# Graph layer with gated attention and a mixture of experts: three small products in float32r with stacked high and low parts

## The chip, the cores and the metric

The kernel runs on one core of a Trainium2 chip. The metric is device time in microseconds; the time of the kernel before is 1862.65 us, the median of three runs (1862.06 to 1864.38).

## The reference, cut to what matters

6250 nodes of 256 features, 100,000 edges of 16 kinds, sorted by target; C = 256.

```
xn = layernorm(x)
gnn = segment_sum(einsum('ni,rio->rno', xn, weight)[rel_type, src] * norm, dst)
q, k, v = xn @ Wqkv ; k = softmax(k over nodes) ; context = k^T v per head (8 heads)
xm = layernorm(xn) * ln_g + ln_b
gate = sigmoid(gelu(xm @ Wg1 + bg1) @ Wg2 + bg2)      # Wg1 256x64, Wg2 64x256
x = x + gnn + (q @ context) * gate @ Wproj + bproj
tokens = layernorm(x)
probs = softmax(tokens @ router_w.T)                  # 8 experts
combine = top 2 of probs, divided by their sum
out = tokens
for e in range(8):
    out = out + combine[:, e] * (gelu(tokens @ w1[e] + b1[e]) @ w2[e] + b2[e])
x = x + out
```

## The kernel before

The nodes are cut into 49 tiles of 128. A large product is made in float32r from operands split into a high part (the value rounded to float32r) and a low part (the rest), as three passes high x high, low x high, high x low: the helper `three` (L1517 to L1526; its matmuls all bear L1524). Three small products are made in plain float32 instead, without a split, and a fourth uses `three`:

- GATES (L1661): the gate hidden `hgp` (64 rows) times `wg2`, two matmuls of 256 columns for a pair of tiles, each of which the trace records twice. It waits for `gap_dve` of the pair before, and ScalarE's GATE_ACT (L901) reads bank 5.
- COMBT and BIAS2 (L1692, L1700): the 8 combine weights of each node (`comb`) are transposed to 8 rows, copied to `ct` by ScalarE (L931), and multiplied with the expert biases `b2s`, one matmul of 256 columns for each tile of the pair, each recorded twice.
- LOGIT (L1685): the normalised tokens times the router, by `three`, six float32r matmuls of 8 columns for each tile. VectorE's TOP (L1403) copies the result out.

**First phase** (to about 900 us): a loop over the tiles. Per tile TensorE transposes the normalised tile, makes key and value (`kv_mm`), the gate's hidden product (64 columns, `hg_mm`), and eight blocks of relations (24 plus 24 matmuls of 512 columns, `gnn_mm`), which ScalarE and VectorE copy in turn to `stage` and SP writes to DRAM as `table`. VectorE scales the hidden product (L1201), ScalarE applies Gelu (L799), TensorE transposes the 64 columns (L1587), ScalarE copies them to `hgt` (L813), and SP stores `hgt` to `hg_d`, ahead of the store of the second half of the table. From tile 24 on, early rows of edges are gathered, split and summed beside it (L1564, L1565; VectorE L1169, L1175, L1190).

**Second phase** (the rest): 24 pairs of tiles and a last single one. All engines go through the same table of eight slots per pair, `SLOTS_OF_PAIR` (L1769): each entry names a step, and each engine carries out, in this order, the steps it has a function for. "+" belongs to the pair one behind, "-" to the pair two behind, "*" to the edges. In each slot TensorE does LAYER1 of one expert (twelve matmuls, `wreg` and `tt`), LAYER2 of another, two behind it (twelve, `ht` and `wreg`), and SUMS, six or four matmuls that sum edge messages (L1645 with the high, L1646 with the low parts). ScalarE makes the high parts of the messages (MSGS, L892), Gelu (L939) and the high part of LAYER1's result (L944). VectorE makes the selection (L1318), the low parts (L1332, L1437), and adds LAYER2's result to the accumulator (ADD, L1451). GATES stands at the end of slot 0, COMBT at the end of slot 2, BIAS2 at the end of slot 5, LOGIT in slot 6 ahead of SUMS. VectorE's COMB in slot 0 ends with L1425, which makes `comb`; in slot 4 MEAN and ScalarE's NORM (L913, L917) stand.

**Setup**: `b2s` and `wg2` are loaded as they are used; ScalarE splits other weights, then begins its first tile with the copies at L795.

## Time and profile before

| | |
|---|---|
| profiled execution | 1848.56 us |
| its span | 1847.0 us |
| TensorE busy | 1726.4 us, 93% |
| VectorE busy | 1352.7 us, 73% |
| ScalarE busy | 958.0 us, 52% |
| GpSimd busy | 1005.4 us, 54% |
| chain that ended last | TensorE 81% of the span, VectorE 5%, ScalarE 3%, issue 6% |

PE is TensorE's matmuls, DVE is VectorE, ACT ScalarE, POOL GpSimd, SP the engine that issues most transfers. Matmuls are pipelined: the duration of one is longer than the distance to the next, and the ends are modelled, so the pace of a block is read from the start of one block to the start of the next. Times in the rows are from the start of the span.

### The profile page before, as it was taken

What the parts mean: (1) busy time and instruction counts of PE and PEld (TensorE: products, weight loads), DVE (VectorE), ACT (ScalarE), POOL (GpSimd) and SP (SyncE); (2) the same over time, 40 slices, a digit from 0 to 9 for tenths busy, and PEclk for the clock granted to TensorE, in tenths of its full rate; (3) what the DMA queues carried; (4) which work ended last, traced back from release to release, by engine and by line L of the source; (5) the groups of instructions that cost most, each with busy time, mean ns of one, the idle gap of its engine ahead of it and who ended that gap; (6) DMA issues with size and microseconds to landing.
All of it is one profiled execution on the core that took longest, in us unless ns stands there. A gap on an engine that the chain in (4) does not pass through costs nothing.

```text
span 1847.0 us, 38898 instructions
## 1 busy us (share of the span) xinstructions
PE 1726.4 (93%) x10903; PEld 1526.2 (83%) x10903; DVE 1352.7 (73%) x3331; ACT 958.0 (52%) x2190; POOL 1005.4 (54%) x1132
## 2 busy tenths in 40 slices
PE   4999999989999999996679999999999999999998
PEld 3788888877778777775569999999999999999998
DVE  5767554466667666764678888888888888888885
ACT  3444222344444444443456666666666666666654
POOL 2233222577777777763366665656565656565630
PEclk9999999999999999997779999999999999999999
DMA  6565564566667666668633232333233333233320
GB/s 201 202 229 214 223 234 189 211 218 218 230 208 240 215 221 225 227 215 297 213 104 103 90 97 87 102 89 97 87 102 89 98 88 100 89 99 90 99 58 12
DMA packets 106583, 286.92 MB, mean 155 GB/s; under 512 B 19719, under 2 KB 41052, under 8 KB 93986
## 3 DMA queue, kind: packets, MB, share of 16 engines
q1 hardware_dynamic: 57762, 166.68, 24.3%
q0 software_dynamic: 40032, 110.39, 21.1%
q10 hardware_dynamic: 8736, 9.20, 1.6%
q8 instruction: 26, 0.43, 0.1%
q14 instruction: 27, 0.22, 0.0%
...
## 4 chain that ended last, share of the span: by engine, by line
PE 81%; issue 6%; DVE 5%; ACT 3%; ACTq 1%; another core or an unknown queue 1%; DMA 1%; DVEq 1%; POOL 0%; SPq 0%; POOLq 0%
PE bank L1524 65%; PE bank L1645 3%; PE bank L1646 2%; PE bank L1564 2%; PE bank L1565 2%; ACT mh L892 2%; PE bank L1706 1%; PE bank L1666 1%; DMA slot<-kv_d 1%; PE bank L1618 1%; ACTq L743 1%; DVE xtp L1372 1%; ACT raw L939 1%; PE bank L1681 1%
## 5 line engine op out<-in xcount | busy, mean ns | idle before, releaser
L709 POOL DMA_INDIRECT stg<-table,idxcur x495 | 507.6, 1025 | 375.6 <-PE bank L1646 189.8
L1524 PE MATMUL bank<-wreg,xt 128*128 128x512 f32 x2352 | 594.8, 404 | 13.6 <-issue 13.2
L1524 PEld LDWEIGHTS bank<-wreg,xt 128*128 128x128 f32 x2352 | 442.2, 193 | 114.0 <-issue 18.8
L609 POOL DMA_INDIRECT raw<-table,idxa x297 | 322.0, 1084 | 119.4 <-issue 72.4
L1524 PE MATMUL bank<-tt,wreg 128*128 128x256 f32 (+1 forms) x2400 | 320.6, 283 | 0.3 <-DVE tt L1398 0.3
L1524 PE MATMUL bank<-wreg,ht 128*128 128x256 f32 x2352 | 319.1, 284 | 0.0
L1524 PEld LDWEIGHTS bank<-tt,wreg 128*128 128x128 f32 x2400 | 298.3, 189 | 8.9 <-issue 6.8
L1524 PEld LDWEIGHTS bank<-wreg,ht 128*128 128x128 f32 x2352 | 294.7, 188 | 8.3 <-issue 8.3
L939 ACT ACTIVATE raw<-bank,cols 128x256 f32<-128x256 f32 (+1 forms) x400 | 163.8, 460 | 195.3 <-PE bank L1524 150.0
L1061 DVE COPY stg<-bank 128x512 f32<-128x512 f32 x196 | 133.9, 685 | 157.3 <-PE bank L1524 132.1
L1332 DVE SCALAR_TENSOR_TENSOR ml<-stg,nrm,mh 128x256 fp32r<-128x256 f32 x495 | 214.7, 480 | 36.7 <-ACT mh L892 33.3
L762 ACT COPY stg<-bank 128x512 f32<-128x512 f32 x196 | 113.1, 581 | 210.8 <-PE bank L1524 154.3
L892 ACT ACTIVATE mh<-stg,nrm 128x256 fp32r<-128x256 f32 x495 | 218.4, 498 | 4.7 <-DVE wreg L1022 1.1
L1451 DVE SCALAR_TENSOR_TENSOR xres<-bank,raw,xres 128x256 f32 (+1 forms) x392 | 170.2, 474 | 50.6 <-PE bank L1524 48.0
L1645 PE MATMUL bank<-mh,sel 128*128 128x256 f32 x495 | 158.3, 335 | 27.3 <-DVE ml L1332 25.3
L785 ACT ACTIVATE mh_a<-raw,nrm 128x256 fp32r<-128x256 f32 x297 | 129.2, 501 | 94.8 <-DMA raw<-table,idxa 71.5
L1437 DVE TENSOR_TENSOR ht<-raw,ht 128x512 fp32r<-128x512 f32 (+1 forms) x200 | 135.6, 678 | 27.2 <-ACT ht L944 27.2
L1175 DVE SCALAR_TENSOR_TENSOR ml_a<-raw,nrm,mh_a 128x256 fp32r<-128x256 f32 x297 | 129.1, 485 | 33.1 <-issue 21.3
L944 ACT CAST ht<-raw 128x512 fp32r<-128x512 f32 (+1 forms) x200 | 122.4, 612 | 38.5 <-PE bank L1524 30.0
L1646 PE MATMUL bank<-ml,sel 128*128 128x256 f32 x495 | 136.6, 287 | 0.0
L1645 PEld LDWEIGHTS bank<-mh,sel 128*128 128x128 f32 x495 | 95.6, 193 | 48.8 <-issue 17.7
L1524 PEld LDWEIGHTS bank<-wkvg,xt 128*128 128x128 f32 x588 | 97.2, 192 | 23.3 <-DVE xt L1065 5.1
...
## 6 DMA issues: line engine op xcount, KB each, us to landing
...
```

What stands on the lines that cost most here:

```text
L609: pool.indirect_dma_start(ring_a[:, r * EARLY + j, :], None, table[0:LIMIT, :], bass.IndirectOffsetOnAxis(ap=idxa[:, at:at + 1], axis=0)). ...
L709: pool.indirect_dma_start(stg[:, (s % 4) * SUP + j, :], None, table, bass.IndirectOffsetOnAxis(ap=idxcur[:, at:at + 1], axis=0)).then_inc( ...
L785: act.activation(mh_a[:, (r % 2) * EARLY + j, :], ring_a[:, r * EARLY + j, :], ACT.Copy, scale=nrm[:, bass.ds(EB * q + j, 1)]).then_inc(hi ...
L892: act.activation(mh[:, (s % 2) * CUT + j, :], stg[:, (s % 4) * SUP + j, :], ACT.Copy, scale=nrm[:, bass.ds(at + j, 1)]).then_inc(msg_hi, 1)
L939: act.activation(hf[e % 2][:, c * 256:c * 256 + nt * P], bank[2 + e % 2][:, c * 256:c * 256 + nt * P], ACT.Gelu, bias=b1c[:, 2 * e + c:2 * ...
L1061: dve.tensor_copy(stage[:, j // 4, (j % 4) * 512:(j % 4 + 1) * 512], bank[3 + j % 4][:]).then_inc(copied(k, j)[0], 1)
L1332: dve.scalar_tensor_tensor(out=ml[:, m, :], in0=stg[:, (s % 4) * SUP + j, :], scalar=nrm[:, bass.ds(at + j, 1)], in1=halves(mh[:, m, :]), ...
L1437: dve.tensor_tensor(ht[e % 2][:, LO, :, 0:n], cols2(hf[e % 2], n), halves(ht[e % 2][:, HI, :, 0:n]), ALU.subtract).then_inc(h_lo, 1)
L1451: dve.scalar_tensor_tensor(out=xk, in0=bank[6 + e % 2][:, a * C:(a + 1) * C], scalar=comb[:, a, e:e + 1], in1=xk, op0=ALU.mult, op1=ALU.ad ...
L1524: mm = pe.matmul(dst, stat(a, c), mov(b, c), start=(n == 0), stop=(n == 3 * chunks - 1))
L1645: pe.matmul(bank[u % 2][:, 0:C], sel[:, m, :], mh[:, m, :], start=(s % 2 == 0 and j == 0), stop=False)
L1646: mm = pe.matmul(bank[u % 2][:, 0:C], sel[:, m, :], ml[:, m, :], start=False, stop=(s % 2 == 1 and j == PART[1] - 1))
```

## The change

The three plain float32 products are made in float32r with split operands, and the router product with fewer matmuls.

- Gate: the hidden tile is doubled by Gelu into 128 columns (64 and the same 64 again), and transposed in one 128x128 transpose. ScalarE writes all 128 rows of `hgt` rounded; VectorE then overwrites rows 64 to 127 with value minus rounded value. `hg_d` and `hgp` have 128 rows. Wg2 is there as `wgh`, rounded, twice in rows, and `wgl`, its rest, 64 rows. GATES is `wgh` with all 128 rows (high and low of the hidden tile at once) and `wgl` with the high 64.
- Expert bias: `c3` holds high, low and high part of `comb` in columns 0, 32 and 64 of 96; COMBT transposes it to 96 rows; `b2h` holds the high part of the biases at rows 0 and 32 and the low part at row 64. BIAS2 is one float32r matmul of 96 rows per tile. New steps are COMB_HI (ScalarE, slot 0) and COMB_LOW (VectorE, the first of slot 1).
- Router: the high and low part of the router weights stand side by side, 16 columns; the high part of the tokens meets both in one matmul, the low part meets the high 8 columns. TOP sums the two halves while it reads them.

The core of the diff; declarations of tensors and semaphores and the renamed counts of waits are left out:

```diff
-            sp.dma_start(b2s[:], b2).then_inc(mixw_in, 16)
-            sp.dma_start(wg2[:], Wg2).then_inc(mixw_in, 16)
+            for n in range(3):
+                sp.dma_start(b2_raw[n * CW:n * CW + X, :], b2).then_inc(late_in, 16)
+            for n in range(2):
+                sp.dma_start(wg2_raw[n * G:n * G + G, :], Wg2).then_inc(late_in, 16)
...
-                act.activation(hgn[:, 1, :], hgn[:, 0, :], ACT.Gelu).then_inc(hg_act, 1)
+                act.activation(hgn[:, 1:3, :], hgn[:, 0:1, :].to_broadcast([P, 2, G]), ACT.Gelu).then_inc(hg_act, 1)
...
-                act.copy(hgt[b][:], bank[2][0:G, 0:P]).then_inc(hgt_cp, 1)
+                if not isinstance(i, int) or i > 0:
+                    act.wait_ge(hgt_cp, k - 1)
+                act.copy(hgt[b][:], bank[2][:, 0:P]).then_inc(hgt_hi, 1)
...
-            act.copy(rwh[:, HI], rwt[:]).then_inc(setup_act, 1)
-            act.wait_ge(mixw_in, 64)
+            act.copy(rwh[:, :, HI], rwt[:]).then_inc(setup_act, 1)
+            act.wait_ge(mixw_in, 32)
             act.copy(wproj[:, HI], wp_raw[:]).then_inc(setup_act, 1)
+            act.wait_ge(late_in, 5 * 16)
+            act.copy(wgh[:], wg2_raw).then_inc(setup_act, 1)
+            act.wait_ge(cleared, 4)
+            for n in range(2):
+                act.copy(b2h[n * CW:n * CW + X, :], b2_raw[n * CW:n * CW + X, :]).then_inc(setup_act, 1)
+            act.copy(b2h[2 * CW:2 * CW + X, :], b2_raw[2 * CW:2 * CW + X, :]).then_inc(setup_act, 1)
...
-                act.copy(ct[:, 0:nt * P], bank[5][0:X, 0:nt * P]).then_inc(ct_act, 1)
+                act.copy(ct[:, 0:nt * P], bank[5][0:3 * CW, 0:nt * P]).then_inc(ct_act, 1)
+
+            def COMB_HI(p, nt):
+                act.wait_ge(comb_dve, p + 1)
+                if not isinstance(p, int) or p > 0:
+                    act.wait_ge(ct_mm, p)
+                if isinstance(p, int) and p == 0:
+                    act.wait_ge(c3_clear, 1)
+                act.copy(c3[:, 0:nt, 0:3:2, 0:X],
+                         comb[:, 0:nt].unsqueeze(2).to_broadcast([P, nt, 2, X])).then_inc(c3_hi, 1)
...
+                dve.tensor_tensor(wgl[:], wg2_raw[0:G], halves(wgh[0:G]), ALU.subtract)
+                low = slice(2 * CW, 2 * CW + X)
+                dve.tensor_tensor(b2h[low, :], b2_raw[low, :], halves(b2h[low, :]), ALU.subtract)
...
+                dve.wait_ge(hgt_hi, k + 1)
+                dve.tensor_tensor(hgt[b][G:2 * G, :], bank[2][G:2 * G, 0:P], halves(hgt[b][G:2 * G, :]),
+                                  ALU.subtract).then_inc(hgt_cp, 1)
...
-                ch.link(dve, dve.tensor_copy(lg[:, 0:nt], bank[5][:, 0:nt * X].rearrange("p (a e) -> p a e", a=nt)))
+                got = bank[5][:, 0:nt * 2 * X].rearrange("p (a h e) -> p a e h", a=nt, h=2)
+                ch.link(dve, dve.tensor_reduce(lg[:, 0:nt], got, AX.X, ALU.add))
...
+            def COMB_LOW(p, nt):
+                dve.wait_ge(c3_hi, p + 1)
+                dve.tensor_tensor(c3[:, 0:nt, 1, 0:X], comb[:, 0:nt], halves(c3[:, 0:nt, 0, 0:X]),
+                                  ALU.subtract).then_inc(c3_lo, 1)
...
-                        pe.transpose(bank[2][0:G, 0:P], hgn[:, 1, :], ident[:]).then_inc(hgt_psum, 1)
+                        pe.transpose(bank[2][:, 0:P], hgn[:, 1:3, :].rearrange("p a g -> p (a g)"),
+                                     ident[:]).then_inc(hgt_psum, 1)
...
-                    mm = pe.matmul(bank[5][:, v * 256:v * 256 + n], wg2[:, v * P:(v + 1) * P],
-                                   hgp[:, 0:nt, :].rearrange("p a n -> p (a n)"), start=True, stop=True)
+                    pe.matmul(bank[5][:, v * 256:v * 256 + n], wgh[:, v * P:(v + 1) * P],
+                              hgp[:, 0:nt, :].rearrange("p a n -> p (a n)"), start=True, stop=False)
+                    mm = pe.matmul(bank[5][:, v * 256:v * 256 + n], wgl[:, v * P:(v + 1) * P],
+                                   hgp[0:G, 0:nt, :].rearrange("p a n -> p (a n)"), start=False, stop=True)
...
-                    mm = three(bank[5][:, a * X:(a + 1) * X], lambda h, c: tt[:, h, c, a * P:(a + 1) * P],
-                               lambda h, c: rwh[:, h, c, :])
+                    at = a * 2 * X
+                    for c in range(CC):
+                        pe.matmul(bank[5][:, at:at + 2 * X], tt[:, HI, c, a * P:(a + 1) * P],
+                                  rwh[:, c].rearrange("p h e -> p (h e)"), start=(c == 0), stop=False)
+                    for c in range(CC):
+                        mm = pe.matmul(bank[5][:, at:at + X], tt[:, LO, c, a * P:(a + 1) * P], rwh[:, c, HI, :],
+                                       start=False, stop=(c == CC - 1))
...
-                pe.wait_ge(comb_dve, p + 1)
+                pe.wait_ge(c3_lo, p + 1)
...
-                    mm = pe.transpose(bank[5][0:X, a * P:(a + 1) * P], comb[:, a, :], ident[:])
+                    mm = pe.transpose(bank[5][0:3 * CW, a * P:(a + 1) * P],
+                                      halves(c3[:, a].rearrange("p n e -> p (n e)")), ident[:])
...
-                    mm = pe.matmul(bank[4][:, a * C:(a + 1) * C], ct[:, a * P:(a + 1) * P], b2s[:],
+                    mm = pe.matmul(bank[4][:, a * C:(a + 1) * C], ct[:, a * P:(a + 1) * P], b2h[:],
                                    start=True, stop=True)
...
 SLOTS_OF_PAIR = (
-    ("-WEIGHT", "*SELECT", "-LOW 1", "*MSGS", "*WINDOW", "-COMB", "-LAYER1 2", "-LAYER2 0", "*SUMS", "+OUT",
+    ("-WEIGHT", "*SELECT", "-LOW 1", "*MSGS", "*WINDOW", "-COMB", "-COMB_HI", "-LAYER1 2", "-LAYER2 0", "*SUMS", "+OUT",
      "+GATES"),
-    ("*SELECT", "-ADD 0", "-LOW 2", "*MSGS", "+GATE_ACT", "+GATE", "-LAYER1 3", "-LAYER2 1", "+GATE_HI", "*SUMS"),
+    ("-COMB_LOW", "*SELECT", "-ADD 0", "-LOW 2", "*MSGS", "+GATE_ACT", "+GATE", "-LAYER1 3", "-LAYER2 1", "+GATE_HI", "*SUMS"),
```

Beside these, VectorE clears `b2h` in the setup (`cleared`) and `c3` once, and the spread of `kmax` (`kmb`) now lies in `dg`, which made it.

## Rows read from the trace of the kernel before

**Rows 1.** The page, part 1: busy us, share of the span, instructions of each engine.
```profile
PE 1726.4 (93%) x10903; PEld 1526.2 (83%) x10903; DVE 1352.7 (73%) x3331; ACT 958.0 (52%) x2190; POOL 1005.4 (54%) x1132
```

**Rows 2.** Stretches: us, PE, PEld, DVE, ACT, POOL busy (x), PEclk, DMA share, GB/s.
```profile
600.00:800.00 200.00, 186.12 (x915) 152.02 (x914) 137.04 (x313) 87.94 (x220) 150.22 (x147) 0.96 0.66 221
...
1300.00:1500.00 200.00, 198.42 (x1533) 186.95 (x1534) 173.12 (x461) 130.21 (x300) 122.31 (x133) 1.00 0.32 95
```

**Rows 3.** Order of time, TensorE, one pair: start, us, line, operation, [idle before].
```profile
1275.96 1.13 PE L1706 MATMUL bank<-b2s,raw 8*128 8x256 f32 x4
1277.02 1.70 PE L1524 MATMUL bank<-wreg,ht 128*128 128x256 f32 x12
1278.55 1.58 PE L1524 MATMUL bank<-tt,wreg 128*128 128x256 f32 x12
1279.97 1.40 PE L1524 MATMUL bank<-rwh,tt 128*128 128x8 f32 x12
1281.23 0.36 PE L1645 MATMUL bank<-mh,sel 128*128 128x256 f32 x1
...
1290.69 1.13 PE L1666 MATMUL bank<-hgp,wg 64*128 64x256 f32 x4
1291.75 1.70 PE L1524 MATMUL bank<-tt,wreg 128*128 128x256 f32 x12
1293.28 1.60 PE L1524 MATMUL bank<-wreg,ht 128*128 128x256 f32 x12
...
1298.46 0.38 PE L1645 MATMUL bank<-mh,sel 128*128 128x256 f32 x1 [0.25 <-DVE ml L1332]
...
1299.88 1.68 PE L1524 MATMUL bank<-wproj,xtp 128*128 128x256 f32 x12
1301.40 0.38 PE L1697 MATMUL bank<-ident,raw 128*8 128x128 f32 x2
1301.54 1.68 PE L1524 MATMUL bank<-tt,wreg 128*128 128x256 f32 x12
...
1312.87 1.13 PE L1706 MATMUL bank<-b2s,raw 8*128 8x256 f32 x4
```

**Rows 4.** The same pair on VectorE.
```profile
1282.39 0.69 DVE L1437 TENSOR_TENSOR ht<-raw,ht 128x512 fp32r<-128x512 f32 x1 [0.35 <-ACT ht L944]
...
1286.60 0.69 DVE L1437 TENSOR_TENSOR ht<-raw,ht 128x512 fp32r<-128x512 f32 x1 [0.43 <-ACT ht L944]
...
1290.39 0.18 DVE L1425 TENSOR_TENSOR raw<-raw 128x16 f32<-128x16 f32 x1
...
1291.67 0.68 DVE L1437 TENSOR_TENSOR ht<-raw,ht 128x512 fp32r<-128x512 f32 x1
...
1293.30 0.69 DVE L1367 SCALAR_TENSOR_TENSOR scr<-gate,bank 128x512 f32<-128x512 f32 x1 [0.16 <-ACT gate L901]
1295.59 0.88 DVE L1451 SCALAR_TENSOR_TENSOR xres<-bank,raw,xres 128x256 f32 x2 [1.61 <-PE bank L1524]
...
1311.48 0.91 DVE L1332 SCALAR_TENSOR_TENSOR ml<-stg,nrm,mh 128x256 fp32r<-128x256 f32 x2 [0.70 <-ACT mh L892]
```

**Rows 5.** The same pair on ScalarE.
```profile
1288.06 0.81 ACT L939 ACTIVATE raw<-bank,cols 128x256 f32<-128x256 f32 x2
...
1292.43 0.84 ACT L901 ACTIVATE gate<-bank,small 128x256 f32<-128x256 f32 x2 [2.09 <-PE bank L1666]
```

**Rows 6.** Order of time, TensorE, in a tile of the first phase.
```profile
252.05 0.38 PE L1533 MATMUL bank<-ident,xn 128*128 128x128 f32 x2
252.27 0.27 PE L1587 MATMUL bank<-ident,hgn 128*64 128x128 f32 x1
252.30 5.85 PE L1524 MATMUL bank<-wreg,xt 128*128 128x512 f32 x24
```

**Rows 7.** Order of time in the setup, ScalarE.
```profile
37.87 1.05 ACT L762 COPY stg<-bank 128x512 f32<-128x512 f32 x2
```

**Rows 8.** The same, TensorE.
```profile
40.22 7.39 PE L1524 MATMUL bank<-wreg,xt 128*128 128x512 f32 x24
```

More of the change, by code:

```diff
@@ L115, in gps_layer @@
         kmax = sb("kmax", [P, C], F32)
-        kmb = sb("kmb", [P, C], F32)
-        wg2 = sb("wg2", [G, C], F32)
+        wgh = sb("wgh", [2 * G, C], F32R)
+        wgl = sb("wgl", [G, C], F32R)
         cols = sb("cols", [P, 32], F32)
         rwt = sb("rwt", [P, CC, X], F32)
-        rwh = sb("rwh", [P, 2, CC, X], F32R)
-        b2s = sb("b2s", [X, C], F32)
+        rwh = sb("rwh", [P, CC, 2, X], F32R)
+        b2h = sb("b2h", [3 * CW, C], F32R)
         iota8 = sb("iota8", [P, X], F32)
@@ L138, in gps_layer @@
             kvs = [sb(f"kvs{b}", [P, KVW], F32, one) for b in range(2)]
-            hgn = sb("hgn", [P, 2, G], F32, one)
-            hgt = [sb(f"hgt{b}", [G, P], F32, one) for b in range(2)]
+            hgn = sb("hgn", [P, 3, G], F32, one)
+            hgt = [sb(f"hgt{b}", [2 * G, P], F32R, one) for b in range(2)]
             bpb = sb("bpb", [P, C], F32, one)
@@ L288, in gps_layer @@
         hgt_psum = sem("hgt_psum")
+        hgt_hi = sem("hgt_hi")
         hgt_cp = sem("hgt_cp")
@@ L1248, in _ @@
             dve.memset(xres[96:P, NT - 1, :], 0.0).then_inc(cleared, 1)
+            dve.memset(halves(b2h[:]), 0.0).then_inc(cleared, 1)
             for k in range(K2):
@@ L1271, in shifts @@
                     dve.wait_ge(kv_in[s], 16 * i + 16)
-                    dve.tensor_tensor(slot[:, s, 0:C], slot[:, s, 0:C], kmb[:], ALU.subtract).then_inc(k_shift, 1)
+                    dve.tensor_tensor(slot[:, s, 0:C], slot[:, s, 0:C], dg[:], ALU.subtract).then_inc(k_shift, 1)
             dve.wait_ge(flag_ready, 1)
@@ L1480, in slot_of @@
                 in_slot(i, s, groups, p1, n1, p2, n2, SELECT=SELECT, MSGS=MSGS, WINDOW=WINDOW, LAST_WINDOW=LAST_WINDOW, GATE=GATE,
-                        GATE_LOW=GATE_LOW, STATS=STATS, MEAN=MEAN, TURN_LOW=TURN_LOW, TOP=TOP, COMB=COMB,
+                        GATE_LOW=GATE_LOW, STATS=STATS, MEAN=MEAN, TURN_LOW=TURN_LOW, TOP=TOP, COMB=COMB, COMB_LOW=COMB_LOW,
                         BIAS2_ADD=BIAS2_ADD, LOW=LOW, ADD=ADD)
```

37 lines of the change are left out of this document (22 added, 15 removed).

## The prediction

> **What bounds the kernel now.** I read the page first, then the table of stretches, then the order of time on TensorE, VectorE and ScalarE inside one pair of the second phase. The reader is to see that TensorE is busy 93% of the span [rows 1], that in a stretch of the second phase it is at 198.4 of 200 us while VectorE is at 173.1 and ScalarE at 130.2, and that in a stretch of the first phase with early sums it is at 186.1 with VectorE at 137.0 [rows 2]. The clock column is 1.00 in the second phase, so its 2.4 GHz level holds and I look for no clock effect there. So the second phase is TensorE's. It takes 36.91 us for a pair of tiles (BIAS2 starts at 1275.96 and next at 1312.87 [rows 3]), and there are 24.5 pairs. But TensorE is not alone at the limit: six SUMS matmuls that start at 1298.46 take until 1299.88, 1.42 us, after an idle 0.25 us, because VectorE's low parts come late [rows 3]. VectorE in its turn idles where TensorE or ScalarE is late: 0.35, 0.43 and 1.61 us [rows 4]. A saving on TensorE counts only if these hand-overs move with it, so both are worked out.
>
> **The change part by part, second phase.** The yardstick is the float32r matmul of 256 columns: twelve from 1278.55 to 1279.97, 0.118 us each [rows 3].
> BIAS2: two plain float32 matmuls (four records) from 1275.96 to 1277.02, 1.06 us; the twelve behind them take 1.53 where 1.42 is usual, 0.11 more, so 1.17 [rows 3]. After: two float32r matmuls of the same 256 columns with 96 rows instead of 8, 0.24. The trace has none of 96 rows; its bounds are 0.24 (as fast as any of 128 rows) and 1.06 (nothing won), and I take the first, to which every float32r row is nearest. Saved 0.93.
> GATES: 1290.69 to 1291.75, 1.06, and 1.53 for the twelve behind, 1.17 in all [rows 3]. After: four float32r matmuls, 0.47. Saved 0.70, bounds 0 and 0.70.
> LOGIT: twelve of 8 columns take 1.26 us, 0.105 each [rows 3], nearly what 256 columns cost, so the load of 128x128 weights sets the pace and not the columns. After: eight with the same loads, 16 columns in four of them. Saved 4 x 0.105 = 0.42; bounds 0 (if 16 columns cost twice 8) and 0.42.
> COMBT: two transposes in 0.14 [rows 3] with 8 weight columns. After: 96 weight columns; two transposes with 128 weight columns take 0.22 [rows 6]. Cost 0 to 0.1, taken at 0.05.
> The sum on TensorE is 0.93 + 0.70 + 0.42 - 0.05 = 2.0 us per pair.
> A rule bears on the first two terms. The trace gives 0.53 us for one float32 matmul of 256 columns. The Trainium skill, "FP8 and Floating Point Precision", TensorE Precision Notes, has true float32 as four passes, and "TensorE: Matmul & The Clock Gate", Architectural detail and Back-to-back issue gap, has a pass at 256/2.4 + 2.5 ns; an estimate from these is 0.44 us, by which BIAS2 would save 0.64 and GATES 0.41, and the sum 1.4 instead of 2.0. The rows decide for 2.0.
>
> **Does it pass the other engines?** I walk one pair with VectorE.
> Up to SELECT of slot 7 nothing on VectorE moves. It then waits 0.35 at L1437 (1282.39) and 0.43 (1286.60) for ScalarE's high parts of experts 0 and 1 [rows 4]; those follow LAYER1 0 and 1, which start 0.93 and 1.35 us earlier, so both waits go, and VectorE reaches COMB 0.8 us earlier.
> There the change adds a chain. COMB's last instruction starts at 1290.39 and takes 0.18 [rows 4]; new are COMB_HI on ScalarE and COMB_LOW, which is VectorE's first instruction of slot 1. VectorE stands idle through ScalarE's copy and two hand-overs. Bounds are 0.2 (that op alone, like the 0.18) and 0.7 (the longest wait for ScalarE in these rows, 1311.48); I take 0.3 of idleness and 0.17 for the subtraction, 0.45 in all. Queued behind the waiting VectorE are SELECT, ADD 0, LOW 2 and the messages of slot 1, and SUMS waits for them. Queued behind ScalarE's COMB_HI are LAYER1 2, the messages of slot 1 and the gate. LAYER1 2 ran at 1288.06, 2.3 us before COMB's last op [rows 4, 5]. COMB now ends at 1290.57 - 0.8 = 1289.8, so LAYER1 2 starts near 1290.0; its Gelus take 0.81 [rows 5] and the high part some 0.6, so that is there near 1291.4. VectorE's LOW 2 started at 1291.67 [rows 4] and comes at 1291.67 - 0.8 + 0.45 = 1291.3, so it waits about 0.1. The gate ran at 1292.43 after a wait [rows 5]; GATES now ends about 2 us earlier, and the gate follows ScalarE's messages, near 1292.3. So this chain costs VectorE 0.45 to 0.65 and takes nothing from TensorE in slots 0 and 1, which needs expert 2's parts only in slot 2.
> Then ADD 1: VectorE is free at 1293.98 (0.69 after 1293.30), and waits 1.61 for LAYER2 1 to 1295.59 [rows 4]. TensorE is 2.0 us earlier there, so ADD 1 starts at 1293.6 if TensorE decides, and at 1293.98 - 0.8 + 0.45 + 0.1 = 1293.7 if VectorE does: both arrive together, 1.9 to 2.0 earlier. From there to the end of slot 5 VectorE had nearly no wait for TensorE, only 0.70 for ScalarE's messages behind NORM (1311.48 [rows 4]), so the rest of the pair moves as a block. The replacement of TOP's copy by a sum over two halves adds 16 elements to a small op, under 0.05. The memory of c3 and the use of dg for kmb are once per run.
> So what TensorE saves passes, with no reserve: 2.0 us per pair. Late next are the SUMS of slot 2 and PROJ, which wait for VectorE as they do now. Over 24.5 pairs this is 49 us.
>
> **First phase.** The gate hidden transpose has 128 weight columns instead of 64. Now it starts 0.22 after the pair ahead of it and the next block starts 0.03 behind it [rows 6], so its weight load hides; I take 0, bounds 0 and 0.08 per tile. ScalarE's Gelu doubles from 64 to 128 columns: hidden, ScalarE is at 88 of 200 [rows 2]. VectorE gets one subtraction of 64x128 from PSUM behind kmax, between the 0.18 of 16 columns (1290.39) and the 0.69 of 512 (1293.30) [rows 4], about 0.3; behind it on VectorE are the early rows and two evacuations, for which TensorE waits. In the first 24 tiles TensorE is saturated and VectorE idle enough. In the 25 tiles with early sums TensorE already loses 7% [rows 2]; bounds are 0 and 0.3 for each, and I take 0.13: 3 us. SP's stores come in the same number; the one of hg_d is twice as wide and waits for VectorE, ahead of the second table store, which is not due until later in the tile.
> Setup: ScalarE gets wgh and three copies for b2h, behind a wait for VectorE's last memsets of the setup; so its table copies of 37.87 come near 41 [rows 7]. TensorE's block at 40.22 needs them, but has 7.39 us for 24 matmuls [rows 8] that take 5.85 elsewhere [rows 6], since VectorE holds it up; so 1.5 of some 3 us are covered, the bounds are 0 and 3, and I take 1. SP issues five small transfers for two ahead of the edge lists, with no one late behind them.
> First phase: +4 us, bounds 0 and 14 (0.08 x 49 + 0.3 x 25 + 3).
>
> **The sum.** The profiled execution took 1848.56 us (span 1847.0). 1848.56 - 49 + 4 = 1803.6. The median of the runs shown is 1862.65, 0.76% above it; in that proportion the forecast is **1817 us**.
>
> **Rivals.**
> A: the hand-over of the combine weights costs more. For it: VectorE arrives at ADD 1 with no reserve, so each further 0.1 us in COMB_HI, LOW 2 or the gate counts in full. Against it: the ops are small. With 1 us lost per pair (the upper bound of the idleness, 0.4 above what I take, and the same again at LOW 2 and the gate), the gain is 24.5 x 1.0 - 4 = 20 us, near 1842.
> B: more than the direct sum comes back. ScalarE waits 2.09 us for the gate and VectorE 1.61 us at ADD 1 just behind the float32 GATES [rows 4, 5], though TensorE's record of LAYER2 1 ends at 1293.28 + 1.60 = 1294.9 [rows 3]; if such late hand-overs hang on the float32 work, SUMS of slot 2 with its 0.7 us too many and 0.25 idle shortens as well. 3.0 us per pair gives 1848.56 - 73 + 4 = 1779.6, near 1793.
> C, the other side: ScalarE's queue. COMB_HI holds LAYER1 2, the messages and the gate for the 2.3 us between 1288.06 and COMB's end. If ScalarE cannot make it up and arrives that much later with the gate, ADD 1 and all behind it, the full 2.3 us fall on the pair against 2.0 saved: +0.3 x 24.5 + 4 = +11, near 1874. It decides once more than about 2 us of the hold reach ADD 1. Against it: ScalarE idled 2.09 us ahead of the gate [rows 5], which takes the hold up.
> D: float32 matmuls cost only the four passes (the 1.4 us per pair above): 1848.56 - 34 + 4, near 1832. Here the mechanism would be that the rest of the 0.53 us is a cost of switching kinds that stays with the remaining float32 transposes; the 0.11 us behind BIAS2 speaks for a switching cost, but of that size only.
>
> **How the numbers follow.** Forecast 0.62, A 0.17, B 0.12, D 0.05, C 0.04. The range reaches from B to just beyond A, 1793 to 1845; what is left out are C and gains above 3 us per pair. Faster by over 0.2% (3.7 us, about what a measurement of this kernel can tell from no change) holds in all but C and a sliver of A: 0.94; same 0.02, slower 0.04.
>
> **What would show it.** BIAS2 start to BIAS2 start at 34.9 us; two BIAS2 records about 0.24 us long together, four GATES in 0.47, eight LOGIT in 0.84, and 1.42 for the block behind each; an idle 0.3 us on VectorE ahead of c3's subtraction; the waits at 1282.39, 1286.60 and 1295.59 gone or under 0.3; ScalarE's L939 of expert 2 behind COMB_HI; VectorE busy over 90% of a second phase stretch. A pair of 36 us, or a VectorE wait of a microsecond in slot 1, would make the prediction wrong on A's side; a first phase that ends 10 us later would break the term of 4 us.

## The result, and the profile after

On the chip of the first measurement the changed kernel took 1852.64 us (median of 4, 1851.96 to 1855.34) beside 1863.52 for the kernel before (median of 4, 1862.06 to 1866.85): 0.9942 of it, 95% interval 0.9925 to 0.9959. That is 0.6% faster, 11 us, where 2.4% or 46 us was predicted; the time lies 8 us above the range. On three further chips the same kernel took 0.985, 0.9851 and 0.9838 of before. So there are two gaps to explain: from 2.4% to 1.5%, which all chips share, and from 1.5% to 0.6%, which only the first chip shows.

The profiled execution took 1855.34 us (span 1853.6). The page's part 1, which answers [rows 1]:
```profile
PE 1706.4 (92%) x10756; PEld 1512.4 (82%) x10756; DVE 1368.3 (74%) x3409; ACT 963.8 (52%) x2219; POOL 1032.9 (56%) x1132
```
TensorE has 20 us less to do, yet in a stretch of the second phase it is now idle for 6 of 200 us, where before it was idle for 1.6 [rows 2]; VectorE's share has not risen. The stretch (columns as in [rows 2]):
```profile
1300.00:1500.00 200.00, 193.85 (x1508) 183.54 (x1508) 172.95 (x469) 129.80 (x305) 127.43 (x131) 1.00 0.33 98
```
One pair on TensorE, in order of time, the blocks that answer [rows 3] (the blocks on line 1564 stand for line 1524 of before):
```profile
1288.95 0.41 PE L1755 MATMUL bank<-b2h,ct 96*128 96x256 f32 x2
1289.19 1.59 PE L1564 MATMUL bank<-wreg,ht 128*128 128x256 f32 x12
1291.60 1.67 PE L1564 MATMUL bank<-tt,wreg 128*128 128x256 f32 x12 [0.81 <-DVE tt L1431]
1293.11 0.28 PE L1733 MATMUL bank<-rwh,tt 128*128 128x16 f32 x2
...
1293.91 0.36 PE L1686 MATMUL bank<-mh,sel 128*128 128x256 f32 x1
...
1303.39 0.28 PE L1707 MATMUL bank<-hgp,wgh 128*128 128x256 f32 x1
1303.60 0.38 PE L1709 MATMUL bank<-hgp,wgl 64*128 64x256 f32 x1
1303.91 0.38 PE L1707 MATMUL bank<-hgp,wgh 128*128 128x256 f32 x1
1304.23 0.38 PE L1709 MATMUL bank<-hgp,wgl 64*128 64x256 f32 x1
1304.54 1.68 PE L1564 MATMUL bank<-tt,wreg 128*128 128x256 f32 x12
1306.05 1.61 PE L1564 MATMUL bank<-wreg,ht 128*128 128x256 f32 x12
...
1325.59 0.41 PE L1755 MATMUL bank<-b2h,ct 96*128 96x256 f32 x2
```
BIAS2 takes 0.24 us (1288.95 to 1289.19) and LOGIT 0.80 (1293.11 to 1293.91), as predicted. (COMBT, the transpose of `c3`, is still plain float32: the change turns two of the plain products into float32r, GATES and BIAS2, and reorders the router's.) GATES takes 1.15 (1303.39 to 1304.54) where 0.47 was predicted and 1.06 stood before. LAYER1 0 waits 0.81 us for TURN_LOW, a wait that did not exist. VectorE in the same pair, with two new waits (1289.52 is ADD 5, 1308.92 is ADD 1):
```profile
1289.52 0.88 DVE L1490 SCALAR_TENSOR_TENSOR xres<-bank,raw,xres 128x256 f32 x2 [0.97 <-PE bank L1564]
1290.32 0.55 DVE L1351 TENSOR_TENSOR sel<-dbl,dpr 128x384 fp32r<-128x384 f32 x1
1290.78 0.68 DVE L1431 TENSOR_TENSOR tt<-bank,tt 128x512 fp32r<-128x512 f32 x1
...
1303.58 0.17 DVE L1463 TENSOR_TENSOR c<-raw,c 128x16 fp32r<-128x16 f32 x1 [0.36 <-ACT c L956]
...
1308.92 0.88 DVE L1490 SCALAR_TENSOR_TENSOR xres<-bank,raw,xres 128x256 f32 x2 [1.67 <-PE bank L1564]
```
The hand-over of the combine weights costs 0.36 + 0.17 us, near the 0.45 predicted. ADD 1's wait, 1.61 before [rows 4], is still there with 1.67, and ADD 5, ahead of TURN_LOW in VectorE's order, has a new one of 0.97. Both follow a TensorE block that had been over for long by its record: LAYER2 5 ran from 1286.91 for 1.68 us, to 1288.59, and ADD 5 starts 0.93 us after that; LAYER2 1 ends at 1306.05 + 1.61 = 1307.66, and ADD 1 starts 1.26 us after that. ScalarE, in the same pair:
```profile
1303.33 0.22 ACT L956 CAST c<-raw 128x32 fp32r<-128x32 f32 x1 [2.52 <-issue]
1303.51 0.84 ACT L965 ACTIVATE raw<-bank,cols 128x256 f32<-128x256 f32 x2
```

### The profile page after: what moved, and what is told of

It reads as the page before. It is cut to its first block, busy times and chain, and to the rows that moved or that the text cites. A ratio compares the mean times of both kernels' runs of the same rounds, so it can differ in the third digit from the quotient of the medians.

```text
span 1853.6 us, 38739 instructions
## 1 busy us (share of the span) xinstructions
PE 1706.4 (92%) x10756; PEld 1512.4 (82%) x10756; DVE 1368.3 (74%) x3409; ACT 963.8 (52%) x2219; POOL 1032.9 (56%) x1132
## 4 chain that ended last, share of the span: by engine, by line
PE 74%; DVE 8%; issue 8%; ACT 3%; DMA 2%; POOL 2%; another core or an unknown queue 1%; ACTq 1%; DVEq 1%; SPq 0%; POOLq 0%
PE bank L1564 60%; PE bank L1686 3%; PE bank L1604 2%; PE bank L1687 2%; PE bank L1605 2%; DMA slot<-kv_d 1%; DVE ml L1365 1%; ACT mh L909 1%; POOL raw L618 1%; ACTq L752 1%; DVE sel L1351 1%; PE bank L1659 1%; DVE xres L1490 1%; DVE xtp L1405 1%
## 5 line engine op out<-in xcount | busy, mean ns | idle before, releaser
L718 POOL DMA_INDIRECT stg<-table,idxcur x495 | 531.5, 1074 | 347.3 <-PE bank L1687 123.4
```

The lines of the kernel that those rows point to most:

```text
L718: pool.indirect_dma_start(stg[:, (s % 4) * SUP + j, :], None, table, bass.IndirectOffsetOnAxis(ap=idxcur[:, at:at + 1], axis=0)).then_inc( ...
```

## The experiments

Sixteen runs were made in four groups, each group on a chip of its own with the kernel before beside it. The kernel before took 1863.5 us on the first chip, 1851.1, 1773.6, 1775.2 and 1850.4 on the second to the fifth, so only ratios are compared across chips. The pair is the distance of two BIAS2 blocks, over 21 pairs of the profile (of the kernel before, 36.87 on the first chip). One execution of each run was profiled.

| kernel | chip | median us | of before [95%] | pair us |
|---|---|---|---|---|
| the changed kernel | 1 | 1852.64 | 0.9942 [0.9925, 0.9959] | 36.59 |
| turn_low_first | 2 | 1826.11 | 0.9873 [0.9846, 0.9900] | 35.79 |
| bias_float32 | 2 | 1825.98 | 0.9862 [0.9836, 0.9889] | 35.95 |
| gate_rows_128 | 2 | 1817.17 | 0.9817 [0.9791, 0.9843] | 35.55 |
| router_alone | 2 | 1836.05 | 0.9911 [0.9882, 0.9940] | 36.13 |
| changed_again | 3 | 1746.91 | 0.9850 [0.9828, 0.9872] | 34.60 |
| first_phase_only | 3 | 1779.41 | 1.0035 [1.0020, 1.0050] | 35.90 |
| gate_float32 | 3 | 1740.88 | 0.9818 [0.9795, 0.9841] | 34.26 |
| select_first_padded | 3 | 1746.34 | 0.9845 [0.9822, 0.9867] | 34.65 |
| changed_third | 4 | 1747.81 | 0.9851 [0.9829, 0.9873] | 34.61 |
| gate_undone | 4 | 1746.77 | 0.9841 [0.9827, 0.9854] | 34.60 |
| gate_rows_again | 4 | 1738.99 | 0.9789 [0.9776, 0.9802] | 34.18 |
| turn_low_again | 4 | 1757.10 | 0.9892 [0.9877, 0.9908] | 35.15 |
| gate_padded | 5 | 1830.34 | 0.9889 [0.9867, 0.9911] | 35.84 |
| small_padded | 5 | 1824.71 | 0.9856 [0.9832, 0.9880] | 35.66 |
| changed_fourth | 5 | 1820.95 | 0.9838 [0.9815, 0.9860] | 35.62 |
| turn_low_third | 5 | 1824.40 | 0.9841 [0.9815, 0.9867] | 35.73 |

**Is it the order ADD 5, SELECT, TURN_LOW?** turn_low_first, turn_low_again and turn_low_third are one kernel:
```
-    ("-ADD 5", "*SELECT", "+TURN_LOW", "-LOW 7", "*MSGS", ...
+    ("*SELECT", "+TURN_LOW", "-ADD 5", "-LOW 7", "*MSGS", ...
```


> The changed kernel with one line of the slot table changed: in slot 6 VectorE does SELECT and TURN_LOW ahead of ADD 5 instead of ADD 5 ahead of both. Theory H (a hand-over took the place of the float32 time): LAYER1 0 waits for TURN_LOW, which stands on VectorE behind ADD 5, and ADD 5 waits for the signal of LAYER2 5; without that the block of LAYER2 6 shrinks from 2.21 us (mean of 20 pairs) to 1.45, a pair goes from 36.6 to 35.8-36.1 us, and the time from 1852.6 to 1834-1842. Rival C (VectorE and ScalarE are simply full, the order does not matter): the pair stays within 0.1 of 36.6 and the time within 3 us of 1852.6.

> The changed kernel with SELECT and TURN_LOW ahead of ADD 5, again, beside the changed kernel itself on one chip. Theory H: it is faster than the changed kernel, by 0.5 to 0.9 us a pair where LAYER1 0 waited (late signals), by nothing elsewhere. Theory L: on a chip with prompt signals it is the same within 0.1% or slower by up to 0.3 us a pair, since MSGS of slots 6 and 0 come later behind TURN_LOW's own wait of 0.8 us.

> The changed kernel with SELECT and TURN_LOW ahead of ADD 5. Where signals are prompt it is slower than the changed kernel by 0.5 us a pair (35.15 against 34.60, 0.9892 of before). On a chip where before takes 1850 or more: Theory H says 0.5 to 0.9 us a pair faster than the changed kernel beside it, since LAYER1 0's wait goes; Theory L says the same loss as elsewhere, and the gap between its 0.9873 and the changed kernel's 0.9942 was the chips'.

The first run looked like a success beside the first chip's 0.9942. Beside the changed kernel on one chip it is none: 0.9892 against 0.9851 on the fourth, 0.9841 against 0.9838 on the fifth, where its pair is 0.11 us longer and Theory L had expected the fourth chip's 0.5. VectorE stands idle at TURN_LOW where it would have done ADD 5; fourth chip, VectorE:
```profile
1074.05 0.55 DVE L1351 TENSOR_TENSOR sel<-dbl,dpr 128x384 fp32r<-128x384 f32 x1
1075.40 0.69 DVE L1431 TENSOR_TENSOR tt<-bank,tt 128x512 fp32r<-128x512 f32 x1 [0.80 <-ACT tt L940]
```
The delay is then in slot 7, where SUMS takes 0.89 us instead of 0.47 (mean of 19 pairs, to the next block's start). So Theory H's cure fails. Its wait is real on every chip, though: the changed kernel on the fourth chip, TURN_LOW on VectorE, then LAYER1 0 on TensorE:
```profile
1209.60 0.68 DVE L1431 TENSOR_TENSOR tt<-bank,tt 128x512 fp32r<-128x512 f32 x1
```
```profile
1210.41 1.69 PE L1564 MATMUL bank<-tt,wreg 128*128 128x256 f32 x12
```
LAYER1 0 starts 0.13 us after TURN_LOW ends. LAYER2 6 ahead of it takes 1.62 instead of the usual 1.42 to 1.44, and LAYER1 0 itself 1.52 instead of 1.41: 0.3 us a pair. With the first chip's late LAYER2 5 this grows to the 0.81 of the pair above.

**The gate product.** gate_rows_128 and gate_rows_again are one kernel, which gives Wg2's low part 128 rows too:
```
-        wgl = sb("wgl", [G, C], F32R)
+        wgl = sb("wgl", [2 * G, C], F32R)
...
-                dve.tensor_tensor(wgl[:], wg2_raw[0:G], halves(wgh[0:G]), ALU.subtract)
+                dve.tensor_tensor(wgl[:], wg2_raw, halves(wgh[:]), ALU.subtract)
...
-                                   hgp[0:G, 0:nt, :].rearrange("p a n -> p (a n)"), start=False, stop=True)
+                                   hgp[:, 0:nt, :].rearrange("p a n -> p (a n)"), start=False, stop=True)
```


> The changed kernel with the low part of Wg2 on all 128 rows, so that all four matmuls of GATES have 128 rows (the added product is low x low, negligible). Theory G: the 0.31 us each of the four comes from the alternation of 128 and 64 rows; now they take 0.12 each, GATES 0.47 instead of 1.15. If TensorE's time in slot 0 passes, the pair falls by 0.68 and the time by 17 to 1836; under H most of it is lost again to the hand-overs in slots 2 and 6, the pair falls by 0-0.3 and the time by 0-8. Rival: the 0.31 us is the price of this product whatever its rows, GATES stays at 1.15 and nothing moves.

> The changed kernel with Wg2's low part on 128 rows times the full stacked hidden layer, again, beside the changed kernel itself on one chip. It took 0.9817 of before on the second chip, with GATES at 0.47 us. Theory S: GATES 1.15 to 0.47, the next block 0.1 less, pair 0.7 to 0.8 shorter than the changed kernel's, so 17 to 19 us: ratio to before 0.975, my predicted 0.9755, where signals are prompt. Rival C (VectorE sets the pair once TensorE has this little): pair at most 0.35 shorter, as in float32 with 128 rows, ratio 0.981, with TensorE waiting for VectorE somewhere.

The added product, low times low, changes no time but its own. The weight loads (PEld) of GATES in changed_third:
```profile
1221.97 0.19 PEld L1707 LDWEIGHTS bank<-hgp,wgh 128*128 128x128 f32 x1
1222.30 0.18 PEld L1709 LDWEIGHTS bank<-hgp,wgl 64*128 64x128 f32 x1
1222.61 0.19 PEld L1707 LDWEIGHTS bank<-hgp,wgh 128*128 128x128 f32 x1
```
The matmuls of the same GATES:
```profile
1222.09 0.28 PE L1707 MATMUL bank<-hgp,wgh 128*128 128x256 f32 x1
1222.30 0.38 PE L1709 MATMUL bank<-hgp,wgl 64*128 64x256 f32 x1
1222.61 0.38 PE L1707 MATMUL bank<-hgp,wgh 128*128 128x256 f32 x1
```
In gate_rows_again, the weight loads:
```profile
1049.56 0.19 PEld L1709 LDWEIGHTS bank<-hgp,wgl 128*128 128x128 f32 x1
1049.68 0.19 PEld L1707 LDWEIGHTS bank<-hgp,wgh 128*128 128x128 f32 x1
```
and the matmuls:
```profile
1049.56 0.28 PE L1707 MATMUL bank<-hgp,wgh 128*128 128x256 f32 x1
1049.68 0.28 PE L1709 MATMUL bank<-hgp,wgl 128*128 128x256 f32 x1
1049.79 0.28 PE L1707 MATMUL bank<-hgp,wgh 128*128 128x256 f32 x1
```
With one row count a load starts a matmul ahead of its own (1049.56 for the matmul of 1049.68) and matmuls follow at 0.12 us. Where the row count changes, load and matmul start together (both 1222.30, both 1222.61) and matmuls follow at 0.31. GATES is then 0.46 us long (1049.56 to 1050.02), just the term of the sum. It is the change of the row count that costs, and not the 64 rows: in the kernel before, the four records of GATES start 0.32, 0.22 and 0.22 us apart, and in gate_float32 below, on 128 rows, 0.22, 0.22 and 0.22. Once the first is through, 64 rows follow each other as fast as 128.

With the 0.1 us that the block behind gets shorter, 0.78 us are saved on TensorE; 0.43 reach the pair (34.61 to 34.18) and 9 us the time. This is rival C of that expectation in part: SUMS of slot 2 takes 1.07 us instead of 0.75 (mean of 19 pairs), since it now waits for VectorE, which has no wait of its own from 1052.92 on. TensorE's SUMS and PROJ in gate_rows_again:
```profile
1056.57 0.28 PE L1687 MATMUL bank<-ml,sel 128*128 128x256 f32 x1
1056.74 0.38 PE L1686 MATMUL bank<-mh,sel 128*128 128x256 f32 x1
1056.97 0.28 PE L1687 MATMUL bank<-ml,sel 128*128 128x256 f32 x1
1057.35 1.68 PE L1564 MATMUL bank<-wproj,xtp 128*128 128x256 f32 x12
```
and VectorE's messages there:
```profile
1055.43 1.26 DVE L1365 SCALAR_TENSOR_TENSOR ml<-stg,nrm,mh 128x256 fp32r<-128x256 f32 x3
1056.62 0.68 DVE L1405 TENSOR_TENSOR xtp<-scr,xtp 128x512 fp32r<-128x512 f32 x1
```
This kernel is the fastest of its group on both chips: 0.9789 of before on the fourth (the changed kernel 0.9851) and 0.9817 on the second.

gate_float32 has the same 128 stacked rows in plain float32, and leaves Wg2's low part out of the product:
```
-                    pe.matmul(bank[5][...], wgh[...], hgp[:, 0:nt, :]..., start=True, stop=False)
-                    mm = pe.matmul(bank[5][...], wgl[...], hgp[0:G, 0:nt, :]..., start=False, stop=True)
+                    mm = pe.matmul(bank[5][...], halves(wgh[...]), halves(hgp[:, 0:nt, :]...), start=True, stop=True)
```


> The changed kernel with GATES as two plain float32 matmuls of 128 rows (stacked Wg2 high against stacked high and low parts of the hidden layer); Wg2's low part is left out of the product. The bias product in float32 on 96 rows took 0.68 us for two (0.34 each), where the kernel before paid 1.06 for two of 8 rows and 1.06 for two of 64 rows (0.53 each). Theory R (a float32 matmul of 256 columns costs 0.53 us on 64 rows or fewer and 0.34 on more): GATES takes 0.68 to 0.75 us instead of 1.15, the pair falls by 0.4 to 36.2 us, time 0.98 to 0.99 of before. Rival Q (float32 costs four passes whatever the rows, 0.42 to 0.53 us each, and the 0.34 came from the next block's start): GATES takes 0.9 to 1.06 us and the time is that of the changed kernel.

TensorE, its GATES and the matmul behind:
```profile
1015.04 1.02 PE L1707 MATMUL bank<-hgp,wgh 128*128 128x256 f32 x4
1015.72 0.47 PE L1564 MATMUL bank<-tt,wreg 128*128 128x256 f32 x1
```
From the start of GATES to the end of the matmul behind it are 1.15 us here, 1.45 in the kernel before on 64 rows (1290.69, and 1291.75 + 0.39), 1.52 in changed_third (1222.09, and 1223.23 + 0.38). So plain float32 on full rows beats the changed form, and the pair shows it (34.26 against 34.60). The next start at 0.68 flatters it, as rival Q has it: four records span 1.02 with the last at 0.38, so they follow at 0.215 us, 0.43 for one float32 matmul. The Trainium skill, "FP8 and Floating Point Precision", TensorE Precision Notes, has true float32 as four passes, from which the prediction estimated 0.44; by that rule, the trace agrees. What the 0.53 of before had on top was the switch of the row count, 128 to 64 or 8 and back.

bias_float32 and select_first_padded (the padded gate weights, the reordering above, and this second one):
```
-                    mm = pe.matmul(bank[4][...], ct[:, a * P:(a + 1) * P], b2h[:], ...
+                    mm = pe.matmul(bank[4][...], halves(ct[:, a * P:(a + 1) * P]), halves(b2h[:]), ...
```
```
-    ("-ADD 1", "*SELECT", "-LOW 3", ...
+    ("*SELECT", "-ADD 1", "-LOW 3", ...
```


> The changed kernel with BIAS2's two matmuls in plain float32 again on the same 96 rows (everything else of the change kept). BIAS2 grows from 0.24 to 1.06 us and the block behind it by 0.1. Theory H: this only fills the time in which LAYER1 0 waits for TURN_LOW, so the pair stays at 36.5-36.9 and the time within 6 us of 1852.6, and LAYER2 5's signal reaches VectorE early again. Rival D (the saving of BIAS2 had passed in full and something else grew): the pair grows by 0.9 us and the time by 22 to 1875.

> The changed kernel with three edits: Wg2's low part on 128 rows with the full stacked hidden layer, SELECT and TURN_LOW ahead of ADD 5 in slot 6, SELECT ahead of ADD 1 in slot 2. Theory H+G (the two losses are separate and add): GATES 0.47 us, LAYER2 6 1.46 us, LAYER2 2 under 1.7 us, so 35.54 (gate weights on 128 rows) less 0.15 and less 0.3 to 0.5: a pair of 35.0 us, time 0.976 of before. Rival C (VectorE, busy 31 of 35.5 us with its own small gaps, sets the pair): 35.5 us and 0.982, as with the gate weights alone; VectorE's wait ahead of ADD 1 or TURN_LOW only moves.

bias_float32 has no changed kernel beside it, so neither of its rivals can be judged by the time; its pair is 0.4 longer than gate_rows_128's. Its BIAS2 starts 0.68 us before the next block, where 1.06 was expected on 96 rows: this miss led to gate_float32. select_first_padded comes out at the changed kernel's time (0.9845 and 0.9850): the two reorderings together lose what the gate weights win. Which of the two loses is not shown there; turn_low_again alone loses 0.54 a pair.

**The parts.** router_alone is the kernel before with the LOGIT and TOP edits. first_phase_only is the kernel before with the first phase's share of the gate edit; its GATES leaves out the low part of the hidden layer. gate_undone takes the whole gate edit back; the core of its diff:
```
-        hgt = [sb(f"hgt{b}", [2 * G, P], F32R, one) for b in range(2)]
+        hgt = [sb(f"hgt{b}", [G, P], F32, one) for b in range(2)]
...
-                act.activation(hgn[:, 1:3, :], hgn[:, 0:1, :].to_broadcast([P, 2, G]), ACT.Gelu).then_inc(hg_act, 1)
+                act.activation(hgn[:, 1, :], hgn[:, 0, :], ACT.Gelu).then_inc(hg_act, 1)
```


> The kernel before with the router part of the change alone (eight matmuls instead of twelve, VectorE sums two halves). LOGIT 1.26 -> 0.81 us. Theory H: nothing in slots 6, 7 and 0 waits for late parts any sooner than before, LAYER1 0 does not start earlier, so the saving passes: pair 36.9 -> 36.5, time 5 to 11 us below the kernel before. Rival C (the other engines are full): pair unchanged, time within 3 us of before.

> The kernel before with only the first-phase part of the gate edit: Gelu written twice, a transpose of 128 columns, the stacked copy to hgt, VectorE's subtraction of rows 64 to 127 and its wait for ScalarE's copy, and stores and loads of 128 rows of hgt. GATES still multiplies rows 0 to 63 in float32, now the rounded high part, so the low part of the hidden gate layer is left out of the output. My prediction put this part at +4 us (bounds 0 and +14). If it holds: ratio 1.002 with tile 12 about 2 us and the last tile about 4 us later than before, the second phase unchanged at 36.85 us a pair. Rival F (the wait for ScalarE's copy and 128-row stores cost more, and are what the changed kernel loses): +10 us or more, ratio 1.005 or more. Rival Z: nothing, 1.000 +- 0.002.

> The changed kernel with the whole gate edit undone: Wg2 and the hidden layer in float32 on 64 rows again, no doubled Gelu, no stacked copy, no subtraction in the first phase, 64-row stores and loads; bias product and router stay changed. Theory S (terms add, TensorE sets the pair): GATES 1.15 to 1.06 us, pair 0.1 us shorter than the changed kernel's, first phase 4 to 6 us shorter: 6 to 9 us below the changed kernel, ratio to before 0.980 to 0.982 on a chip with prompt signals. Then the gate edit as written is a loss. Rival T (the first phase's cost is hidden, GATES no dearer than before where the data comes from): within 2 us of the changed kernel.

The router edit alone gives 0.9% [0.6, 1.2] on the second chip, more than its 0.42 us a pair (10 us, 0.55%): the pair is 0.7 shorter than before's on the first chip, but no pair of before was profiled on the second. The first phase's share costs 0.35%, 6.2 us, with an interval of 3.5 to 8.9.

Undoing the whole gate edit leaves the pair as it is (34.60 and 34.61). The reason stands on TensorE, in OUT (`xtp` and `wqc`), the block just ahead of GATES; gate_undone, then changed_third, whose GATES starts at 1222.09 as shown above:
```profile
1215.21 1.57 PE L1554 MATMUL bank<-xtp,wqc 128*128 128x256 f32 x12
1216.72 1.13 PE L1697 MATMUL bank<-hgp,wg 64*128 64x256 f32 x4
```
```profile
1220.68 1.57 PE L1564 MATMUL bank<-xtp,wqc 128*128 128x256 f32 x12
```
Ahead of a GATES that begins with 64 rows OUT takes 1.51 us, ahead of one that begins with 128 it takes 1.41. That gives back the 0.09 by which GATES itself is longer (1.15 against 1.06). So the gate edit gains nothing on TensorE. Whether the first phase's cost then remains, the medians do not tell: they are 1.0 us apart (0.9841 and 0.9851), with intervals of 2.4 and 3.9 us to either side, too wide to tell rival T's 2 us from Theory S's 6. The profiled executions are 5.9 us apart, 5.5 of them before the first BIAS2 (926.2 against 931.7).

**Prompt and late hand-overs.** changed_again, changed_third and changed_fourth are the changed kernel unedited.

> The changed kernel itself, unedited, on the chip of the runs beside it. On its first chip it took 0.9942 of the kernel before. Three of its edited copies took 0.9873 (TURN_LOW ahead of ADD 5), 0.9862 (bias product in float32) and 0.9817 (gate weights on 128 rows) on a second chip. Theory H (it loses time in its own order of waits, at LAYER1 0 behind TURN_LOW): the same kernel shows the same here, 0.994 +- 0.003, pairs of 36.6 us that swing by 1.5 us, LAYER1 0's wait ahead of it, and so a time clearly above those copies. Rival N (what set it apart was the chip or the one profiled execution): a ratio of 0.987 or less, steady pairs near 35.9 us and no wait ahead of LAYER1 0.

> The changed kernel unedited, beside the three below. So far: 0.9942 of before on a first chip (pairs of 36.6 us against 36.87), 0.985 on a third chip, where both kernels ran 5% faster (pairs of 34.60 against 35.89). In the third chip's traces every semaphore signal of TensorE came about 0.3 us behind its block; in those of the first, behind a third of the blocks, it came 0.6 to 4 us behind. Theory L (late signals of TensorE, and nothing in the kernel's order, take the rest of the gain): if the time of before is near 1773 us here, signals are prompt and the ratio is 0.985 with steady pairs; if it is near 1850 to 1863, signals are late and the ratio is 0.988 to 0.994. Theory H (the order ADD 5, SELECT, TURN_LOW): LAYER1 0 waits for TURN_LOW on any chip.

> The changed kernel unedited, as baseline of this chip. If before takes about 1773 us: 0.985, pairs of 34.60 us. If before takes 1850 or more: signals of TensorE up to 4 us late, pairs of 36 to 36.6 us, ratio 0.988 to 0.994.

On the fourth chip, ADD 1 and ADD 5 on VectorE (LAYER2 1 and 5 on TensorE start at 1224.74 and 1241.23 there and take 1.61 and 1.69), and the stretch:
```profile
1226.50 0.88 DVE L1490 SCALAR_TENSOR_TENSOR xres<-bank,raw,xres 128x256 f32 x2 [0.40 <-PE bank L1564]
```
```profile
1243.05 0.88 DVE L1490 SCALAR_TENSOR_TENSOR xres<-bank,raw,xres 128x256 f32 x2 [0.17 <-PE bank L1564]
```
```profile
1300.00:1500.00 200.00, 199.88 (x1597) 193.02 (x1595) 183.13 (x502) 137.69 (x321) 135.66 (x141) 1.00 0.35 104
```
ADD 1 and ADD 5 start 0.15 and 0.13 us after the blocks' recorded ends, where on the first chip it was 1.26 and 0.93. What VectorE waited for TensorE ahead of all ADDs (us, times), over 22 pairs: the kernel before and the changed kernel on the first chip, then the changed kernel on the fifth and on the fourth:
```profile
  PE bank L1524: 30.8, 39
```
```profile
  PE bank L1564: 33.2, 33
  remote: 11.2, 6
```
```profile
  PE bank L1564: 13.9, 36
```
```profile
  PE bank L1564: 9.4, 35
```
So with prompt hand-overs TensorE is full (199.9 of 200 us) and VectorE at 91.6%. The semaphores' events in the traces show the same: over 21 pairs, of those that could be matched, 28% of TensorE's signals in the kernel before and 33% in the changed one came more than 0.5 us after the recorded end of the matmul that gives them, and 31% in changed_fourth; on the third and fourth chip none did.

The mean of 19 pairs, us from a block's start to the next block's, shows where the pair gets longer (the number behind a name is the chip):

| | before, 1 | changed, 1 | first_phase_only, 3 | changed_again, 3 | changed_fourth, 5 | gate_padded, 5 |
|---|---|---|---|---|---|---|
| LAYER2 6, up to LAYER1 0 | 1.54 | 2.20 | 1.54 | 1.61 | 1.61 | 1.56 |
| OUT | 1.50 | 1.56 | 1.50 | 1.41 | 1.43 | 1.41 |
| GATES | 1.06 | 1.16 | 1.06 | 1.15 | 1.15 | 0.67 |
| LAYER2 2 and SUMS, slot 2 | 3.21 | 3.25 | 2.19 | 2.19 | 2.85 | 3.36 |

Slot 2 loses 1.0 us on the first chip, before the change as much as after it, and nothing on the third. Of what only the changed kernel loses on the first chip, the largest part is 0.6 us ahead of LAYER1 0. There ADD 5 starts 0.77 us after LAYER2 5's recorded end in the mean; in the kernel before, and in changed_fourth, it is 0.14.

The fifth chip is as slow as the first for the kernel before within 0.7%, and still the changed kernel gets 0.9838 there. Rival N of that expectation holds: the 0.9942 was met on one chip of four, and is not the kernel's order alone. Of Theory L the prompt side holds; its late side (0.988 to 0.994) fails on the fifth chip, where signals are late and the ratio is 0.9838.

**Padding alone.** gate_padded is gate_undone with rows of zeros from 64 to 128 in Wg2 and in the hidden layer's buffer; small_padded is router_alone with the same and with the bias product's operands padded from 8 to 96 rows, nothing stacked:
```
-        wg2 = sb("wg2", [G, C], F32)
+        wg2 = sb("wg2", [2 * G, C], F32)
...
-        b2s = sb("b2s", [X, C], F32)
+        b2s = sb("b2s", [3 * CW, C], F32)
```


> The changed kernel with the gate edit undone, and Wg2 and the hidden layer's buffer of the second phase padded with rows of zeros from 64 to 128, cleared once: the product is the float32 one of the kernel before, on 128 rows. Theory R (a float32 matmul of 256 columns takes 0.53 us on 64 rows and 0.34 on 128): GATES 0.67 where the 64-row form takes 1.06, pair 34.2 to 34.3, without the first phase's doubled work: where signals are prompt 8 us below the changed kernel, ratio to before 0.979 to 0.981. Rival Q (the 0.34 came from the data, zeros and the like, or VectorE sets the pair below 34.6): GATES 1.06, or GATES 0.67 and a pair still of 34.6, and a time within 2 us of the changed kernel.

> The kernel before with the router edit, and with its two small float32 products merely padded with zero rows (gate product to 128 rows, bias product from 8 to 96): nothing is split into high and low parts, no hand-over of the combine weights, no work added to the first phase. Theory R: BIAS2 0.68 instead of 1.06 and 0.24 in the changed kernel, GATES 0.67, LOGIT 0.81; TensorE's sum is before's less 0.38, 0.39 and 0.44 = 1.2 us a pair, 34.7 us, and VectorE and ScalarE have 0.45 and 0.22 us less to do than in the changed kernel: ratio to before 0.983 to 0.985, as much as the changed kernel got. Rival C (VectorE's work sets the pair): below 34.5 us and faster than the changed kernel.

BIAS2 of small_padded and the matmul behind it, on TensorE:
```profile
1016.68 1.03 PE L1722 MATMUL bank<-b2s,ct 96*128 96x256 f32 x4
1017.36 0.47 PE L1533 MATMUL bank<-wreg,ht 128*128 128x256 f32 x1
```
From BIAS2's start to the end of the next matmul are 1.15 us, as in gate_float32, where the 8-row form of before takes more: its next matmul only starts after 1.06 [rows 3]. So the direction of Theory R holds for 8 rows too; its price of 0.34 does not, since the block behind two such matmuls gets 0.19 us longer (its second matmul starts 0.30 after its first instead of 0.12).
The times do not settle more: small_padded, with no splitting, no hand-over and no first phase work, is within the interval of the changed kernel (0.9856 and 0.9838), and gate_padded is slower (0.9889) though it does less: its GATES has 0.67, and slot 2 takes 3.36 us where changed_fourth has 2.85 (table above). Neither Theory R's 0.979 to 0.981 nor rival Q's equal time came. Both ran only on the fifth chip, where a good part of the hand-overs is late; what padding is worth where they are prompt is not shown.

## Why the prediction was wrong

- **BIAS2 and LOGIT**: right. 0.24 and 0.80 us where 0.24 and 0.84 were predicted, and 96 rows count as 128 do. What the walk missed is that the 0.93 saved brings TensorE to LAYER1 0 before TURN_LOW is done, even on the chips with prompt hand-overs: 0.3 us a pair.
- **GATES**: the step that failed everywhere. The term "after: four float32r matmuls, 0.47, saved 0.70" was mis-sized: it measured 1.15, because two of the four have 64 rows between neighbours of 128, and with the 0.09 that OUT gets shorter it saves nothing. gate_rows_again has the 0.46. With 128 rows throughout the time falls by 9 us, half of the 17 that lie between 2.4% and 1.5%; the other half does not pass VectorE (next point).
- **"What TensorE saves passes, with no reserve"**: right where hand-overs are prompt. The sum with GATES corrected is 2.0 - 0.7 = 1.3 us a pair; measured between the third chip's first_phase_only, whose second phase is the kernel before's in time, and changed_again: 35.90 - 34.60 = 1.30. That they agree to the hundredth is luck: the 0.3 at LAYER1 0 is made up by several savings under 0.1 us each that the sum did not have, as in the block ahead of BIAS2 (0.61 and 0.53). It ends soon after: with 0.78 less on TensorE, 0.43 arrive, and VectorE's slot 2 decides.
- **ADD 1's wait "goes"**: nearly right where hand-overs are prompt: in the mean of 19 pairs it falls from 1.27 us (first_phase_only) to 0.34 (changed_again), the rest being what GATES failed to save. It failed on the first chip (1.37 and 1.42). The walk moved ADD 1's start by what TensorE saves ahead of it, and so took the time between TensorE's recorded end and VectorE's start for constant. It was 0.7 us before (1295.59 against 1294.9, [rows 4] and [rows 3]) and is 1.26 after, in the mean 0.79 and 1.20. With the order ADD 5, SELECT, TURN_LOW a late LAYER2 5 reaches LAYER1 0 (0.81 us). The pair fell by 0.28 instead of 1.3. The first chip's share of the miss is thus located, but its cause is not shown.
- **Hand-over of the combine weights**: 0.36 of idleness for 0.3, 0.17 as taken. The two waits at L1437 are gone. Rivals A and C fell; ScalarE still idles 2.52 ahead of COMB_HI.
- **Rival B**: the excess of SUMS in slot 2 does not hang on the float32 work. first_phase_only has the float32 GATES and BIAS2 and no excess (0.75 us for SUMS); the changed kernel on the first chip has it as before (1.37 and 1.41).
- **First phase +4 us**: mis-sized, within its bounds of 0 and 14. The gate's share was taken at 3 and measured 6.2, interval 3.5 to 8.9. In the first chip's profiled executions the first BIAS2 starts at 996.0 against 980.9 before, 15 us later and past the 10 that the prediction named as breaking this term. One execution of each does not settle it: before's profiled one lies 14 to 15 us under its median, and on the second chip four kernels start BIAS2 between 979.9 and 988.9, router_alone, which has no first phase work, at 985.3. Of the setup, the copies came when expected, near 41, but TensorE's block of 24 is 1.1 us later and takes 8.59 against 7.39, 2.3 in all where 1 was taken (ScalarE, then TensorE; [rows 7, 8]):
```profile
40.73 1.05 ACT L771 COPY stg<-bank 128x512 f32<-128x512 f32 x2
```
```profile
41.34 8.59 PE L1564 MATMUL bank<-wreg,xt 128*128 128x512 f32 x24
```
- **Rival D**: its price of 0.43 for one float32 matmul was right, its rest was a switching cost, but of row counts, and it went with BIAS2's rows and stayed with GATES'. Its 1832 us are 0.984 of before, what three chips show; that is luck, since it had BIAS2 save 0.64 and GATES 0.41, where BIAS2 saved 0.93 and GATES nothing.

What stays open: why TensorE's hand-overs come late on some chips, whether its records or its signals are off there, and why the changed kernel met them worse on the first chip than on the fifth, where as many come late. No run here changes that alone, and the changed kernel was measured on the first chip in one series only.
